# Perceiver layers, last self-attention: two chunks times both row halves per unit, and output products in three float32r parts spread over the units

## What is computed

```
q = einsum('qdh,bcd->bhcq', Q, x) * sq        # 16 heads of 64
k = einsum('qdh,bcd->bhcq', K, x) * sq
v = einsum('vdh,bcd->bhcv', V, x) * sv
att = where(causal, einsum('bhcq,bhCq->bhcC', q, k) / d_query, -inf)
p = softmax(att)
y = einsum('bhcC,bhCv->bhcv', p, v)
z = einsum('dvh,bhcv->bcd', W, y) * (sqrt(d_embed / d_value) / num_heads)
x = x + z
```

## Time and profile before

| | us |
|---|---|
| median of 3 runs | 1840.79 |
| lowest, highest | 1831.35, 1844.19 |
| the profiled execution's own time | 1835.99 |
| its span in the trace | 1833.7 |
| TensorE busy in the span | 1703.6 (93%) |

### The profile page before, as it was taken

The page is one execution under the profiler, slowest core; times in us unless marked ns, Lnnn a source line. Parts: engine busy times, 40 slices in busy tenths (PEclk is TensorE's granted clock), DMA queues, the critical chain, the costliest instruction groups (busy, mean ns, idle before and its releaser), DMA issues. The chain is left out here.

```text
span 1833.7 us, 23193 instructions
## 1 busy us (share of the span) xinstructions
PE 1703.6 (93%) x8830; PEld 1316.8 (72%) x8830; DVE 991.7 (54%) x1526; ACT 581.0 (32%) x1054; POOL 339.3 (19%) x294
## 2 busy tenths in 40 slices
PE   7899999999998989987999988989799999999996
PEld 4899999999994777753565656558687665676672
DVE  1669677687673634465899997474523440000014
ACT  4353444443522111112344432034245511111110
POOL 0521432133200010022355542100100020000010
PEclk9899999999998989988798989989898989999998
DMA  4322133213113567736163550430100086696960
GB/s 130 108 91 72 55 108 93 70 54 109 55 40 131 197 246 254 255 117 240 54 223 113 171 208 1 153 140 1 66 28 1 1 286 238 224 341 226 322 233 29
DMA packets 112898, 251.36 MB, mean 137 GB/s; under 512 B 14710, under 2 KB 44294, under 8 KB 108038
## 3 DMA queue, kind: packets, MB, share of 16 engines
q1 hardware_dynamic: 104208, 230.65, 36.3%
q10 hardware_dynamic: 6006, 10.62, 1.7%
q0 software_dynamic: 2560, 8.39, 1.4%
HBM read 230.89 MB, written 18.75 MB: 136 GB/s over the span
## 5 line engine op out<-in xcount | busy, mean ns | idle before, releaser
L374 PE MATMUL x_s_ps<-x_cxt,x_qs 128*128 128x400 f32 (+1 forms) x1152 | 246.0, 359 | 9.5 <-POOL x_qs L347 5.4
L400 PE MATMUL x_o_ps<-x_cx,x_pt 128*128 128x386 f32 (+1 forms) x1248 | 230.3, 343 | 0.0
L1129 PEld LDWEIGHTS e_ps<-e_xg,e_w 128*128 128x128 f32 x1792 | 206.6, 192 | 32.7 <-issue 32.5
L400 PEld LDWEIGHTS x_o_ps<-x_cx,x_pt 128*128 128x128 f32 (+1 forms) x1248 | 220.6, 190 | 1.4
L1129 PE MATMUL e_ps<-e_xg,e_w 128*128 128x128 f32 x1792 | 209.2, 276 | 6.6 <-issue 5.8
L374 PEld LDWEIGHTS x_s_ps<-x_cxt,x_qs 128*128 128x128 f32 x1152 | 207.1, 192 | 10.8 <-issue 10.6
L1121 PE MATMUL e_ps<-e_w,xt 128*128 128x512 f32 x352 | 160.5, 597 | 0.9 <-DMA e_w<-in_L_ffn_W 0.9
L2228 PE MATMUL x_s_ps<-x_cxt,x_qs 128*128 128x512 f32 (+1 forms) x384 | 144.0, 533 | 7.8 <-POOL x_qs L2424 5.8
L2228 PEld LDWEIGHTS x_s_ps<-x_cxt,x_qs 128*128 128x128 f32 x384 | 69.1, 197 | 85.8 <-issue 79.9
L450 DVE TENSOR_TENSOR x_pt<-x_t_ps,x_pt 128x512 fp32r<-128x512 f32 (+1 forms) x128 | 74.7, 586 | 92.6 <-ACT x_pt L540 92.1
L1364 DVE TENSOR_TENSOR e_y<-e_ps,e_b 128x512 f32<-128x512 f32 x20 | 13.7, 686 | 202.7 <-PE e_ps L1121 202.7
(11 more groups left out here) (390 smaller groups left out, 2696.7 us busy)
## 6 DMA issues: line engine op xcount, KB each, us to landing
e_w<-in_L_ffn_W SPq DMA_DIRECT2D x16, 4096.0 KB, 16.2
x_cxt<-in_ctxT SPq DMA_DIRECT2D x8, 2401.5 KB, 8.7
x_cx<-in_ctx SPq DMA_DIRECT2D x8, 2304.0 KB
e_w<-in_L_ffn_gate_up_proj SPq DMA_DIRECT2D x8, 2048.0 KB, 8.1
x_stage<-in_ctxT SPq DMA_DIRECT2D x16, 768.0 KB, 4.4
x_stage<-in_ctx SPq DMA_DIRECT2D x16, 768.0 KB, 6.3
e_w<-in_L_ffn_down_proj SPq DMA_DIRECT2D x8, 1024.0 KB, 8.8
ff_w<-in_L_xattn_W SPq DMA_DIRECT2D x2, 4096.0 KB, 17.2
```

What stands on the lines that cost most here:

```text
L374: last = nc.tensor.matmul(s_ps[:, n, 0:b - a], qs[:, u % 2, p, c, :], cxt[:, q, c, a:b], start=(m + c == 0), stop=(m + c == len(PARTS) + C ...
L400: last = nc.tensor.matmul(o_ps[:, 0:WIDE], pt[0:rows, p, t, :], cx[0:rows, q, t, :], start=(t + m == 0), stop=(t + m == KT - 1 + len(PARTS ...
L1129: last = nc.tensor.matmul(u_ps[:, g % 2, a * PER + n, :], w1[:, e % PAIR, m, a * hidden + c * P:a * hidden + (c + 1) * P], xg[:, m, :], st ...
```

## The change

A unit's four heads are now two chunks (2g and 2g+1) times both halves. In S the two halves alternate, and go to two PSUM banks (`s_bank` is 0 or 2, plus the half); W likewise alternates between PSUM partitions 0 to 63 and 64 to 127 of one bank, 6. Each of the four heads now counts up its semaphore. W's result is one block of 128 partitions by 256 columns: ScalarE rounds it to float32r (`yt` high part), VectorE forms the low part in the new `result_low(u)`, which stands between `lowered(u+1)` and `normal(u)` for unit u-2. Since W has one bank, W(u) waits until `result_low(u-1)` has read it.

`project(u)` now runs for each unit, over its two chunks: six float32r matmuls that add to bank 7 over the four units of a tile. It stands last in TensorE's round, for unit u-2. The output weights are split as well: ScalarE makes the high parts in four pieces between copies of values, into the space that held the value weights; GpSimd makes the low parts in four pieces after the last value product. P(0) to P(3) wait for one piece each.

S(0) and S(1) stand before the last three value products, and `exponent(0)` before their copies. The mask is loaded twice, for two heads side by side.

```diff
-        s_bank, t_bank, y_bank, z_bank = (0, 1), (2, 3), (4, 5), 6
+        s_bank, t_bank, y_bank, z_bank = (0, 2), (4, 5), 6, 7
+        N_V = 2 * TT
+        BEHIND = 3
...
-                    lo = (g % 2) * DH
-                    for k in range(G):
-                        c = (g // 2) * G + k
-                        last = nc.tensor.matmul(ps[:, s_bank[u % 2], k * P:(k + 1) * P], qk[lo:lo + DH, 0, c, t * P:(t + 1) * P],
-                                                qk[lo:lo + DH, 1, c, t * P:(t + 1) * P], start=True, stop=True)
-                    last.then_inc(s_ready, 1)
+                    for j in range(2):
+                        for half in range(2):
+                            c, lo = 2 * g + j, half * DH
+                            last = nc.tensor.matmul(ps[:, s_bank[u % 2] + half, j * P:(j + 1) * P], qk[lo:lo + DH, 0, c, t * P:(t + 1) * P],
+                                                    qk[lo:lo + DH, 1, c, t * P:(t + 1) * P], start=True, stop=True)
+                            last.then_inc(s_ready, 1)
...
-                    if u >= 2:
-                        pe.wait_ge(yt_ready, u - 1)
-                    lo = (g % 2) * DH
-                    for k in range(G):
-                        h = 2 * ((g // 2) * G + k) + g % 2
-                        last = nc.tensor.matmul(ps[lo:lo + DH, y_bank[u % 2], k * P:(k + 1) * P],
-                                                v[:, t, h * DH:(h + 1) * DH], pt[:, u % 2, k, :], start=True, stop=True)
-                    last.then_inc(y_ready, 1)
-
-                def project(t):
-                    pe.wait_ge(yt_ready, (t + 1) * NG)
-                    if t >= 1:
+                    if u >= 1:
+                        pe.wait_ge(yl_ready, u)
+                    for j in range(2):
+                        for half in range(2):
+                            h, lo = 2 * (2 * g + j) + half, half * DH
+                            last = nc.tensor.matmul(ps[lo:lo + DH, y_bank, j * P:(j + 1) * P],
+                                                    v[:, t, h * DH:(h + 1) * DH], pt[:, u % 2, 2 * half + j, :], start=True, stop=True)
+                            last.then_inc(y_ready, 1)
+
+                def project(u):
+                    t, g = u // NG, u % NG
+                    if u < NG:
+                        pe.wait_ge(zl_ready, g + 1)
+                    pe.wait_ge(yl_ready, u + 1)
+                    if g == 0 and t >= 1:
                         pe.wait_ge(z_used, t)
-                    for c in range(HC):
-                        last = nc.tensor.matmul(ps[:, z_bank, :], yt[:, t % 2, c, :], wz[:, c, :], start=(c == 0), stop=(c == HC - 1))
+                    for c in (2 * g, 2 * g + 1):
+                        for p, q in PARTS:
+                            last = nc.tensor.matmul(ps[:, z_bank, :], yt[:, p, c, :], output_part(q)[:, c, :],
+                                                    start=(c == 0 and p + q == 0), stop=(c == HC - 1 and q == 1))
                     last.then_inc(z_ready, 1)
...
+                def result_low(u):
+                    part = slice(2 * (u % NG), 2 * (u % NG) + 2)
+                    dve.wait_ge(yh_ready, u + 1)
+                    nc.vector.tensor_tensor(yt[:, 1, part, :], ps[:, y_bank, 0:2 * P].rearrange("p (j n) -> p j n", j=2),
+                                            yt[:, 0, part, :].bitcast(F32), ALU.subtract).then_inc(yl_ready, 1)
+
                 lowered(0)
                 for u in range(U):
                     if u + 1 < U:
                         lowered(u + 1)
+                    if u >= 2:
+                        result_low(u - 2)
                     normal(u)
```

More of the change, by code:

```diff
@@ L1634, in self_attention_L1 @@
         wz = core.sb(ctx, "s1_wz", [P, HC, D])
-        mask = core.sb(ctx, "s1_mask", [P, P])
+        mask = core.sb(ctx, "s1_mask", [P, 2 * P])
         qk = core.sb(ctx, "s1_qk", [P, 2, HC, TOK])
@@ L1658, in value_part, with output_part @@
             return ws[:, :, :, :, :].rearrange("p r a c n -> p (r a c n)").rearrange("p (a c n) -> p a c n", a=2, c=KC)[:, part, :, :]
+        def output_part(part):
+            if part == 0:
+                return vs[:, :, :, :].rearrange("p a c n -> p (a c) n")
+            return ws[:, :, :, :, :].rearrange("p r a c n -> p (r a c n)").rearrange("p (c n) -> p c n", c=HC)
         with nc.Block() as block:
@@ L1663, in _ @@
                 sp.dma_start(wv[:, :, :], w["L1_attn_V"].rearrange("(c p) n -> p c n", p=P)).then_inc(in_v, 16)
-                sp.dma_start(mask[:, :], w["mask_L1"]).then_inc(in_m, 16)
+                for j in range(2):
+                    sp.dma_start(mask[:, j * P:(j + 1) * P], w["mask_L1"]).then_inc(in_m, 16)
                 sp.dma_start(wz[:, :, :], w["L1_attn_W"].rearrange("(c p) n -> p c n", p=P)).then_inc(in_m, 16)
@@ L1679, in _, with values @@
                     last.then_inc(p_ready, 1)
-                for n in range(2 * TT):
+                def values(n):
                     half, t = n // TT, n % TT
@@ L1688, in _ @@
                     last.then_inc(p_ready, 1)
-                pe.wait_ge(p_used, 2 * HC + 2 * TT)
                 def scores(u):
@@ L1728, in project @@
                     last.then_inc(z_ready, 1)
-                pe.wait_ge(in_m, 32)
+                for n in range(N_V - BEHIND):
+                    values(n)
+                pe.wait_ge(p_used, 2 * HC + 4)
+                pe.wait_ge(in_m, 48)
                 scores(0)
                 scores(1)
+                for n in range(N_V - BEHIND, N_V):
+                    values(n)
+                pe.wait_ge(p_used, 2 * HC + N_V)
                 for u in range(U + 2):
@@ L1739, in _ @@
                         weigh(u - 1)
-                    if u >= 2 and (u - 2) % NG == NG - 1:
-                        project((u - 2) // NG)
+                    if u >= 2:
+                        project(u - 2)
             @block.scalar
@@ L1765, in _, with value_copy @@
                 nc.scalar.copy(value_part(0, 1), wv[:, :, 512:1024]).then_inc(vh_ready, 1)
-                for n in range(2 * TT):
+                def value_copy(n):
                     half, t = n // TT, n % TT
@@ L1769, in _, with output_high @@
                     nc.scalar.copy(v[:, t, half * 512:(half + 1) * 512], ps[:, n % 8, :]).then_inc(p_used, 1)
+                def output_high(n):
+                    act.wait_ge(in_m, 48)
+                    nc.scalar.copy(output_part(0)[:, 2 * n:2 * n + 2, :], wz[:, 2 * n:2 * n + 2, :]).then_inc(zh_ready, 1)
                 def exponent(u):
@@ L1776, in exponent @@
                     last.then_inc(exp_ready, 1)
+                for n in range(TT):
+                    value_copy(n)
+                output_high(0)
+                output_high(1)
+                value_copy(TT)
+                output_high(2)
+                output_high(3)
                 exponent(0)
+                for n in range(TT + 1, N_V):
+                    value_copy(n)
                 for u in range(U + 1):
@@ L1784, in _, with add @@
                         if u >= 2:
-                            act.wait_ge(y_ready, u - 1)
+                            act.wait_ge(y_ready, G * (u - 1))
                         nc.scalar.copy(pt[:, u % 2, :, :], ps[:, t_bank[u % 2], :].rearrange("p (g n) -> p g n", g=G)).then_inc(pt_ready, 1)
                     if u >= 1:
[L1788 to L1794, removed]
+                        g = (u - 1) % NG
+                        act.wait_ge(y_ready, G * u)
+                        if u - 1 >= NG:
+                            act.wait_ge(z_ready, u - NG)
+                        nc.scalar.copy(yt[:, 0, 2 * g:2 * g + 2, :],
+                                       ps[:, y_bank, 0:2 * P].rearrange("p (j n) -> p j n", j=2)).then_inc(yh_ready, 1)
+            @block.gpsimd
+            def _(pool):
+                pool.wait_ge(p_ready, 2 * HC + N_V)
+                for n in range(NG):
+                    part = slice(2 * n, 2 * n + 2)
+                    pool.wait_ge(zh_ready, n + 1)
+                    nc.gpsimd.tensor_tensor(output_part(1)[:, part, :], wz[:, part, :], output_part(0)[:, part, :].bitcast(F32),
+                                            ALU.subtract).then_inc(zl_ready, 1)
             @block.vector
             def _(dve):
-                def add(dve, t):
-                    dve.wait_ge(z_ready, t + 1)
+                def add(t):
+                    dve.wait_ge(z_ready, (t + 1) * NG)
                     nc.vector.scalar_tensor_tensor(x[:, t, :], ps[:, z_bank, :], z_scale, x[:, t, :],
@@ L1842, in _ @@
                         lowered(u + 1)
+                    if u >= 2:
+                        result_low(u - 2)
                     normal(u)
-                    if u >= NG + 2 and (u - 2) % NG == 0:
-                        add(dve, (u - 2) // NG - 1)
-                add(dve, TT - 1)
+                    if u >= NG + 2 and u % NG == 2:
```

(4 more changed lines are left out.)

17 lines of the change are left out of this document (10 added, 7 removed).

## The result

| us | before | after |
|---|---|---|
| median | 1841.29 | 1818.25 |
| lowest, highest (4 runs each) | 1831.35, 1844.19 | 1814.24, 1821.17 |
| the profiled execution | 1835.99 | 1815.60 |
| its span | 1833.7 | 1813.8 |
| first value matmul to the end of the last addition ("the stage") | 104.3 | 87.0 |

The ratio is 0.989, with a 95% interval of 0.986 to 0.993: about 1.1% faster, 20 us (23 between the medians). The time of the whole kernel moves by more than the effects looked for here (19 executions of the kernel before took from 1819 to 1843), while a stage's length in the trace repeats: the changed kernel gave 87.04 and 87.08 in two profiles, the kernel of e2 80.66 both times. So the experiments are read by stage length; those of f6, f7, f9 and f10 come from one execution each.

The account below looks back on a forecast made before the run. TensorE was taken as the bound, busy 1703.6 of 1833.7 us. The loop's terms summed to 58.3 against 82.4, 24.1 less; minus 3.5 for the clock, 20.6 less gave 1817 us, range 1807 to 1835.

Parts of the forecast that it names:

- The total: Whole kernel: 1817 us, from a stage 20.6 us shorter, with everything behind it moving by as much.
- S and W: Loop rounds: the array's two halves overlap, S 1.09 to 0.64 and W 1.02 to 0.58 us, saving 7.2 and 7.0.
- a limit of issue: TensorE's queue at 0.034 us an instruction: S 0.78, W 0.72, taking 4.5 us from the gain; not adopted.
- strict program order: The Trainium skill's rule for matmul start and end: S and W 0.11 us longer each, sum 3.5 us smaller; not adopted.
- Its pair: S(0) and S(1) before, on different halves: 1.71 us together, 2.05 if in line; taken as evidence of overlap.
- P: Output projection in each round: six float32r matmuls, 1.56 us; sixteen take 25.0 where four took 28.2.
- The end: Last rounds: T(14) and T(15), with no S ahead, wait 0.32 us each; P(15) then takes 1.56 and 0.8.
- The start: First rounds: T(1) waits 1.17 and T(2) 1.24 us; GpSimd's low parts are ready before P(0) to P(3), so hidden.
- The clock: Loop start: waits of 0.68, 1.17 and 1.24 bring 8.5 us of low clock; 3.5 us taken off the gain.
- the halves do run at once: Rival denied this for S and W: they stay at 1.09 and 1.02, 10 us less, 1828; chance 0.16.
- the chain through `result_low`: Rival: this chain bounds the round, 0.3 us beyond TensorE's 3.36; 16 to 19 less, 1821; chance 0.08.
- the low clock was shorter than before: Rival held the opposite: it lasts 17 us again, 7.8 come back, 16 less, 1822; chance 0.14.

Follow-up runs that it names:

- e2: The changed kernel with the output weights' low parts formed early by VectorE, in a buffer of their own: stage 80.66 us against 87.0.
- f6: The kernel of e1 with P as two float32 products over its two chunks instead of six float32r ones: stage 85.2 us against 80.7.
- f7: The kernel of e1 with S and W not alternating, each half's two products standing together: stage 81.1 us against 80.7.
- f9: The kernel of e1 with S(0), S(1) and exponent(0) back behind the value products: stage 84.3 us against 80.7.
- f10: The kernel of e1 with S reading partitions 0 to 63 for all heads, so that S cannot overlap: stage 86.8 us against 80.7.
- e1: The changed kernel with GpSimd forming the low parts early, during value products 5 to 7, in a buffer of their own: stage 80.7 us against 87.0.
- e4: The kernel before with only the alternating halves and one bank for W; P and late S(0), S(1) as before: stage 91.6 us against 104.3.
- e8: The kernel of e1 with exponent(1) and normal(1) also ahead of the last value copies: stage 82.1 us against 80.7.
- e3: The changed kernel with S(0), S(1) and exponent(0) again behind all value products and their copies: stage 88.5 us against 87.0.

## Why the prediction was right, and where it was not

**The total**, 1817 against a median of 1818.25, fell closer than its steps deserve. In the trace the stage gave back 17.3 us where the sum said 20.6. The rest of the span's 19.9 is in parts that the change does not touch: the stage began 6.1 us earlier (1360.26 against 1366.40) and what follows it took 3.5 us longer (366.5 against 363.0). The same parts moved by as much and more among the experiments (the stage began at 1360.3 to 1376.0). So the nearness of the total is in part luck.

**S and W** were right: 0.65 and 0.59, predicted 0.64 and 0.58. f10 shows it by undoing it, and f7 that the bound for a limit of issue (0.78 and 0.72) was needless for this size. The prediction held that its rows could not tell its own count of slots from that of strict program order. Its pair could: in strict order S(1) could start only with the last of S(0)'s eight matmuls and the pair would show 2.05 - 0.11 = 1.94, where the row has 1.71. Why S(1) started half-way through S(0) in before is thereby explained only so far: four matmuls ahead in the queue don't hold the other half back, eight do.

**P** was right: 1.58 for 1.56. **The round**: 3.40 for 3.36, with TensorE as the bound from the fourth on, and no wait for GpSimd at P.

**The end**: T(14) and T(15) waited 0.18 and 0.17 for the 0.32 predicted; the cast was 0.37 and not 0.42.

**The start** was the step that failed. The sentence "Hidden" about GpSimd's low parts asked only whether P waits for them; it does not. (GpSimd's parts took 2.35 each for the 2.14 put in, and were done 2.7 before P(0).) It did not ask what GpSimd's work does to VectorE, on whose `normal` T waits. T(1) waited 2.72 where 1.17 was predicted, T(2) 2.56 for 1.24: 2.9 us, and the loop came out at 63.8, or 64.9 with the 1.1 of S(0) and S(1) that now stand ahead, for 61.8. Without the hold-up, e1 gives 57.4 + 1.1 = 58.5, where the sum without its clock term said 58.3. So the sum was right for a kernel in which the low parts stand elsewhere.

**The clock**: it fell, as forecast, for 10.2 us where 8.5 were put in. But the reason given was that waits of 0.68, 1.17 and 1.24 would leave TensorE too idle; e1 has waits of 0.68, 1.12 and 1.12 and no fall. In after the clock fell at 1389.8, behind T(1)'s wait of 2.72 and ahead of T(2)'s, so it was GpSimd's hold-up that brought it on. Why a fall comes with one set of waits and not with another, and what sets its length, stays open: in before the clock had fallen at 1392.7, when only 0.5 of the wait of 2.19 (1392.16 to 1394.35) was over, and lasted 17.0, while e4, with nearly the same waits, had 6.8. A right size for a wrong reason, and so luck: the allowance of 3.5 us happened to stand in for about half of a contention that I had not seen and that cost 6.4 (e1).

**The rivals**: the halves do run at once, the chain through `result_low` stayed below TensorE's round, and the low clock was shorter than before. What W's four semaphore increments cost by themselves no run here shows.

## What to carry to other kernels

Work put on an idle engine is hidden only if it also leaves the engines beside it alone: look which VectorE operations on the path have both inputs in SBUF before GpSimd is given a long one at the same time. Overlapping two halves of TensorE's array shortens its work only as far as something else fills the round: here a third of the gain depended on spreading another stage's matmuls into it. A wait at the head of a dense TensorE loop should be priced with the low clock that may come with it: here from nothing (e1, waits of 1.12) to three times the wait (before).

## What the runs showed of the hardware that was not expected

- A VectorE TENSOR_TENSOR of 128x512 with both inputs in SBUF took 2.29 and 2.65 us beside GpSimd's TENSOR_TENSOR of 128x1024 (2.35 us each) instead of 0.69, ending 0.54 and 0.55 behind it; the GpSimd operation behind the first took 2.81.
- Four loads and matmuls of one half standing ahead of the other half's don't delay it: S is 0.65 in either order.
- Waits of 1.12 twice within 4.1 us left the granted clock at 1.00 (e1, e2); one of 2.17 (e8), 2.53 (f9) or 2.62 (e4) each time came with a stretch at 0.50, of 3.4 or 6.8 us, and one of 2.72 (after) or 4.55 (e3) with 10.2. Before, with 2.19, had 17.0, and the clock fell 0.5 into that wait.
